# Silu of keys and queries on ScalarE, two tiles to a function table, and a logits bias on TensorE

## The chip, the cores and the metric

The kernel runs on one core of a Trainium2 chip. The metric is the device time of one execution in microseconds. A core has TensorE (PE, matrix products), VectorE (DVE), ScalarE (ACT, activation functions), GpSimd (POOL) and SyncE (SP, which here only starts transfers), and 16 DMA engines. Each engine executes its own instructions in order, and they meet at semaphores.

## The reference, cut to what matters

The input is 8 sequences of 512 tokens of width 256. All arithmetic is in float32.

```
xn = layernorm(x)
# attention branch, 16 heads of 16
q = silu(xn @ Wq)            k = l2_norm(silu(xn @ Wk))       v = xn @ Wv
gamma = -sigmoid(xn @ Wgamma)          f = sigmoid(xn @ Wf1 @ Wf2)
a = k * gamma * f
for each token:  S = S * f ;  sab = a . S ;  S = S + k (sab + v) ;  o = q . S
s = layernorm(o * sigmoid(xn @ Wog1 @ Wog2)) * norm_w @ Wo
# expert branch, 8 experts, top 2
logits = xn @ Wg + bg
out = sum over the two chosen experts of weight * (gelu(xn @ W1 + b1) @ W2 + b2)
g = silu(layernorm(out) * gamma + beta)
result = x + s * g
```

## The kernel before

The 4096 tokens are 32 tiles of 128 partitions; a tile holds 16 consecutive tokens of each of the 8 sequences. The recurrence runs the other way round: 128 partitions hold 8 sequences times 16 heads, and the 512 tokens are taken two by two, as 256 pairs `g`. Eight pairs form a chunk, which is exactly what one tile delivers. Four stages follow each other.

**Head.** Tiles 0 to 3 are projected with nothing beside them.

**Woven stage.** VectorE works the recurrence (`two_steps`), and each of its first pairs carries the VectorE work of one more tile: the pair `g` carries tile `g + 4`. I call such a pair with its tile a slot, and name it by its tile. In a slot VectorE does, in this order: `silu(tile)` (L1009: the product of the projected keys and queries in PSUM, `psA`, with their sigmoid `sg`, into the record `rec`), two wide products and a sum of the recurrence (L1167, L1170, L1172), three more small groups of it, then `scale_k(tile - 1)` (L1024), `square_sums(tile)` (L1015: logits plus their bias; L1019: sums of squares of the keys), then the end of the pair with `scale_a(tile - 1)` (L1031) in it. `scale_a` completes the record of a tile, and SyncE then stores it (`spill`, L368, 768 KB). The stored records come back in the recurrence's layout as chunks (`load_chunk`, L371). SyncE's queue, in order, is for each tile: spill, for the first three a wait for its landing and the load of the chunk, and then a block of zeros (L388) for the expert branch's buffer `xs_d`.

For each tile the other engines do this. TensorE: transposes of the next tile (L827), the low-rank product (L835), keys and queries into `psA` (L841), values, gammas and logits into `psB` (L847), forget and output gates into `psF` (L853). ScalarE (`silus`): normalises the tile after next (`normal`, L624), copies the low-rank product (L646) and the next tile's transposes (L632), takes the sigmoid of `psA` (L652), of gamma (L658), copies the values (L659), takes the sigmoid of the gates (L661), squares the forget gate (L664) and squares the keys (L668). GpSimd (`factors`): forget gate squared times gamma (L474), a maximum (L477), and the power -1/2 (L481) that gives the keys' inverse norm.

`psA`, `psB`, `psF`, the squares and most factors are double-buffered, so tile n waits for tile n-2; the ring `rec` has four places, so tile n waits on `s_recd` until the spill of tile n-4 has landed.

**Routing and scatter.** When slot 32 is done VectorE selects the experts (`route`, L1098 is its last line), GpSimd scatters all token rows to their experts in 64 indirect transfers (L499), and VectorE works on through the recurrence alone up to pair 55.

**Experts beside the shared recurrence.** From pair 56 on GpSimd makes half of the products of each pair (L312, L329), and between pairs it lands the expert outputs in memory (L527) when ScalarE has written them (L719). TensorE runs 39 expert tiles (L887, L899). From pair 224 on, each pair also carries one tile of the output stage (L533 is its first GpSimd step of the expert branch's norm).

The bias of the second expert layer is added by a product of a row of ones with the bias (L901), and the change uses that form.

Of the kernel before, what the change touches and what calls it, by code (L numbers as in the profile page):

```python
# [11 lines left out]
P = 128  # L12
# [41 lines left out]
def build(nc, x, wq, wk, wv, wgamma, wf1, wf2, wog1, wog2, norm_w, wo,  # L54
          wg, bg, w1, b1, w2, b2, gamma, beta, out):
    ctx = ExitStack()
    with ctx:
# [53 lines left out]
        sg = work[:, o1:o1 + 4 * D].rearrange("p (u n) -> p u n", u=2)  # L111
        f2 = work[:, o1 + 4 * D:o1 + 6 * D].rearrange("p (u n) -> p u n", u=2)
        ksq = work[:, o1 + 6 * D:o1 + 7 * D]
# [79 lines left out]
        s_sg = sem("s_sg")  # L193
# [249 lines left out]
        def _(pool):  # L443
# [27 lines left out]
            def factors(n, u, first, last):  # L471
                pool.wait_ge(s_f2, n + 1)
                pool.wait_ge(s_gam, n + 1)
                pool.tensor_tensor(f2[:, u, :].rearrange("p (h c) -> p h c", h=H), f2[:, u, :].rearrange("p (h c) -> p h c", h=H),  # L474
                                   gam[:, u, :].unsqueeze(2).broadcast_to([P, H, HD]), ALU.mult).then_inc(s_fg, 1)
# [5 lines left out]
                pool.tensor_tensor(rinv[:, u, :], ssm[:, u, :], neghalf[:, 0:H], ALU.pow).then_inc(s_ng, 1)  # L481

# [138 lines left out]
        def _(act):  # L621
# [5 lines left out]
            def turned(n, u, first):  # L627
                act.wait_ge(s_T, n + 1)
                if not first:
                    act.wait_ge(s_L, n - 1)  # L630
                    act.wait_ge(s_Bp, n - 1)
                act.activation(xTs[u][:, :, :], psT[u][:, 0:D].rearrange("p (c t) -> p c t", c=KC), ACT.Copy)\  # L632
                    .then_inc(s_xTs, 1)
# [4 lines left out]
            def silus(n, u4, first, last):  # L638
                u = u4 % 2
                first, last, no_record = first and u4 < 2, last and u4 >= RS - 2, first  # L640
                if not last:
                    normal(n + 2)
                act.wait_ge(s_L, n + 1)
                if not first:
                    act.wait_ge(s_Fp, n - 1)
                act.activation(t1[u][:, :], psT[u][0:2 * HD, D:D + P], ACT.Copy).then_inc(s_t1, 1)  # L646
                if not (last and u == 1):
                    turned(n + 1, (u + 1) % 2, first and u == 0)
                act.wait_ge(s_A, n + 1)
                if not first:  # L650
                    act.wait_ge(s_kq, n - 1)
                act.activation(sg[:, u, :], psA[u][:, :], ACT.Sigmoid).then_inc(s_sg, 1)  # L652
                act.wait_ge(s_Bp, n + 1)
                if not first:
                    act.wait_ge(s_rec, n - 1)
                if not no_record:
                    act.wait_ge(s_recd[u4], (n // RS) * 16)
# [656 lines left out]
```

## Time and profile before

| | us |
|---|---|
| median of 3 runs (lowest, highest) | 1235.33 (1234.92, 1239.51) |
| profiled execution, its own time | 1241.86 |
| its span | 1240.1 |
| busy: PE, DVE, ACT, POOL | 941.8, 1122.2, 398.0, 933.0 |
| mean granted clock of TensorE | 0.866 |

The span is the time from the first to the last recorded instruction; busy is the sum over an engine's instructions. VectorE is busy for 90% of the span. The granted clock is 1 at 2.4 GHz and 0.5 at 1.2 GHz. In the timeline views a row begins with its start and its duration in microseconds, and the brackets at its end give the idle time in front of it and what ended that. Two instructions of one engine overlap a little, so the step from start to start is the price of one, and not its duration.

### The profile page before, as it was taken

The numbers are of one execution on the slowest core, as the hardware profiler recorded it, in microseconds if no ns is written. First come the engines' busy times: TensorE is split into PE (matmuls) and PEld (weight loads), VectorE is DVE, ScalarE is ACT, GpSimd is POOL, SyncE is SP. The second block draws the span as 40 slices with busy tenths as digits, with TensorE's granted clock in tenths as the row PEclk, the third lists the DMA queues.
The fourth block names the chain that finished last, engine by engine and source line by source line (L and its number), as shares of the span: only waits on it lengthen the run. The fifth ranks groups of instructions, "written<-read, shape, count | busy, mean of one in ns | idle before, by whom it ended". The sixth has DMA issues, their size and how long they took to land.

```text
span 1240.1 us, 17339 instructions
## 1 busy us (share of the span) xinstructions
PE 941.8 (76%) x3773; PEld 686.6 (55%) x3774; DVE 1122.2 (90%) x3478; ACT 398.0 (32%) x1015; POOL 933.0 (75%) x926
## 2 busy tenths in 40 slices
PE   5888888200019999999999999999999952667663
PEld 2333333100017778888787878887888841445442
DVE  3789999999999999999999999899999999978882
ACT  3444544200003232233223333332332213454552
POOL 3766666447753888888888888888888888777763
PEclk9788989655559999999999999999999985676777
DMA  5565655464333566666566666666666453443322
GB/s 163 171 226 178 188 201 190 147 211 114 108 107 119 174 190 200 195 199 189 181 188 192 199 201 185 185 192 199 199 199 192 131 150 101 111 135 117 83 68 56
DMA packets 238034, 202.59 MB, mean 163 GB/s; under 512 B 140401, under 2 KB 216017, under 8 KB 237969
## 3 DMA queue, kind: packets, MB, share of 16 engines
q1 hardware_dynamic: 160930, 82.81, 25.5%
q10 hardware_dynamic: 70224, 100.49, 24.4%
q0 software_dynamic: 6816, 18.69, 4.5%
q14 instruction: 54, 0.44, 0.1%
q8 instruction: 10, 0.16, 0.1%
HBM read 139.42 MB, written 62.54 MB: 163 GB/s over the span
## 4 chain that ended last, share of the span: by engine, by line
PE 56%; DVE 17%; POOL 8%; DMA 7%; issue 6%; ACT 4%; SPq 3%; ACTq 0%; DVEq 0%; POOLq 0%
PE psF L899 22%; PE psA L887 20%; POOL xs_d L499 6%; PE psA L955 4%; PE psF L901 4%; DMA rec_d<-work 3%; PE psF L917 2%; DMA work<-xs_d 2%; DVE obh L1156 2%; SPq L337 2%; DVE ubuf L1172 1%; PE psT L875 1%; DVE prod_a L1167 1%; DVE work L1009 1%; PE psT L949 1%
## 5 line engine op out<-in xcount | busy, mean ns | idle before, releaser
L312 POOL TENSOR_TENSOR prod_a<-state,rbh 128x512 f32<-128x512 f32 x200 | 254.4, 1272 | 94.0 <-DVE state L1227 68.8
L899 PE MATMUL psF<-wts,work 128*128 128x256 f32 x1248 | 290.0, 386 | 2.3 <-ACT work L708 1.2
L887 PE MATMUL psA<-xT,wts 128*128 128x256 f32 x1248 | 281.9, 385 | 1.3 <-ACT xT L702 0.8
L887 PEld LDWEIGHTS psA<-xT,wts 128*128 128x128 f32 x1248 | 235.6, 191 | 45.0 <-issue 13.8
L899 PEld LDWEIGHTS psF<-wts,work 128*128 128x128 f32 x1248 | 232.3, 191 | 48.1 <-issue 16.8
L329 POOL TENSOR_TENSOR prod_q<-state,rbh 128x512 f32<-128x512 f32 x175 | 221.9, 1268 | 0.0
L1156 DVE TENSOR_REDUCE obh<-prod_q 128x16 f32<-128x272 f32 x512 | 218.7, 428 | 0.0
L708 ACT ACTIVATE work<-psA,b_sb 128x256 f32<-128x256 f32 x312 | 130.7, 470 | 162.4 <-PE psA L887 159.0
L1214 DVE TENSOR_REDUCE ubuf<-prod_a 128x16 f32<-128x272 f32 x200 | 86.1, 431 | 46.5 <-POOL prod_a L312 46.4
L719 ACT ACTIVATE work<-psF,work 128x256 f32<-128x256 f32 x78 | 36.9, 473 | 256.8 <-PE psF L901 245.7
L875 PE MATMUL psT<-ident,work 128*128 128x128 f32 x156 | 24.2, 279 | 118.2 <-DMA work<-xs_d 118.2
L481 POOL TENSOR_TENSOR rinv<-ssm,neghalf 128x16 f32<-128x16 f32 x32 | 100.7, 3148 | 2.7
L499 POOL DMA_INDIRECT xs_d<-x_acc,idx x64 | 79.0, 1234 | 19.5 <-issue 18.9
L527 POOL DMA_INDIRECT y_d<-work,ids x78 | 78.9, 1011 | 14.6 <-issue 12.6
L1227 DVE TENSOR_TENSOR state<-psB,outer 128x256 f32<-128x256 f32 x200 | 84.4, 422 | 5.8
L1206 DVE TENSOR_TENSOR prod_a<-state,psT 128x256 f32<-128x256 f32 x200 | 83.9, 420 | 6.0
L875 PEld LDWEIGHTS psT<-ident,work 128*128 128x128 f32 x156 | 19.3, 143 | 123.9 <-issue 115.3
L1209 DVE TENSOR_REDUCE psB<-prod_a 128x16 f32<-128x272 f32 x200 | 86.8, 434 | 0.0
L1220 DVE TENSOR_TENSOR psB<-prod_a,psB 128x256 f32<-128x256 f32 x200 | 83.8, 419 | 0.0
L1212 DVE TENSOR_TENSOR psB<-rbh,psB 128x256 f32<-128x256 f32 x200 | 83.7, 419 | 0.0
L1222 DVE TENSOR_TENSOR outer<-rbh,psB 128x256 f32<-128x256 f32 x200 | 83.0, 415 | 0.0
L841 PE MATMUL psA<-w_kq,xT 128*128 128x512 f32 x128 | 78.9, 749 | 0.0
(171 smaller groups left out, 1564.0 us busy)
## 6 DMA issues: line engine op xcount, KB each, us to landing
wts<-in_L_ffn_W_dram ACTq DMA_DIRECT2D x78, 1024.0 KB, 5.4
rec_d<-work SPq DMA_DIRECT2D x32, 768.0 KB
rbh<-rec_d SPq DMA_DIRECT2D x32, 768.0 KB, 5.6
xs_d<-zero SPq DMA_DIRECT2D x26, 387.0 KB, 9.2
work<-xs_d ACTq DMA_DIRECT2D x39, 258.0 KB, 5.6
wts<-y_d ACTq DMA_DIRECT2D x16, 512.0 KB, 5.7
x_acc<-in_L_attn_x_dram SPq DMA_DIRECT2D x32, 128.0 KB
o_d<-obh SPq DMA_DIRECT2D x32, 128.0 KB, 7.3
```

The costliest lines, as they stand in the source:

```text
L312: eng.tensor_tensor(prod_a[:, n, 1:3, :, 0:HD], state[:, g % SR, :, :].unsqueeze(1).broadcast_to(wide), rows.unsqueeze(2).broadcast_to(wid ...
L329: eng.tensor_tensor(prod_q[:, g % SR, :, :, 0:HD], state[:, g % SR, :, :].unsqueeze(1).broadcast_to(wide), rbh[:, u, 2 * n - 1:2 * n + 1, ...
L481: pool.tensor_tensor(rinv[:, u, :], ssm[:, u, :], neghalf[:, 0:H], ALU.pow).then_inc(s_ng, 1)
L499: pool.indirect_dma_start(xs_d, bass.IndirectOffsetOnAxis(idx[:, 2 * n + c:2 * n + c + 1], 0), x_acc[:, n, :], None).then_inc(s_sc, 16)
L708: act.activation(hT[:, m, :], psA[m // 2 % 2][:, m % 2 * MT:(m % 2 + 1) * MT], ACT.Gelu, bias=b1_sb[:, bass.ds(e * FC + m, 1)]).then_inc(s ...
L887: mm = pe.matmul(psA[m // 2 % 2][:, m % 2 * MT:(m % 2 + 1) * MT], w1_sb[v][:, c, m * P:(m + 1) * P], xgT[:, c, :], start=(c == 0), stop=(c ...
L899: pe.matmul(psF[q][:, 0:D], hT[:, m, q * P:(q + 1) * P], w2_sb[v][:, m, :], start=(m == 0), stop=False)
L1156: dve.tensor_reduce(obh[:, c % OB, row % RING, :], prod_q[:, g % SR, side, :, :], AX.X, ALU.add).then_inc(s_o, 1)
L1206: dve.tensor_tensor(prod_a[:, n, 0, :, 0:HD], old, over_v(home_a[:, n, :]), ALU.mult).then_inc(s_chain, 1)
L1209: dve.tensor_reduce(u1, prod_a[:, n, 0, :, :], AX.X, ALU.add).then_inc(s_chain, 1)
L1214: dve.tensor_reduce(raw, prod_a[:, n, 2, :, :], AX.X, ALU.add).then_inc(s_chain, 1)
L1227: dve.tensor_tensor(new, home_o, outer[:, 1, :, :], ALU.add).then_inc(s_chain, 1)
```

## The change

VectorE's `silu` and its semaphore go. ScalarE takes the Silu of `psA` itself and writes it to the record (after: L652), and squares the keys behind it (L657). Silu and Sigmoid lie in different function tables, so ScalarE reloads its table (ACT_TABLE_LOAD) between them. To share the reloads the tiles go in groups: tile 0, then 1 and 2, 3 and 4, up to 29 and 30, then 31. In a group the silus of both tiles come first (`ahead`, `silu_kq`), and then the sigmoids of both (`sigmoids`). The loop over tiles is written out. The squares get a second buffer.

The logits' bias becomes a product on TensorE, a row of ones times `bg_bc`, 128x8, added to `psB` (after: L856), and ScalarE copies the logits out (L666). GpSimd makes the inverse norm first and the product with gamma last (L471, L475, then L478). On VectorE `square_sums(tile)` now stands ahead of `scale_k(tile - 1)`.

```diff
 POOL, factors(n):
-                pool.wait_ge(s_f2, n + 1)
-                pool.wait_ge(s_gam, n + 1)
-                pool.tensor_tensor(f2[:, u, :]..., gam..., ALU.mult).then_inc(s_fg, 1)
                 pool.wait_ge(s_ss, n + 1)
                 pool.tensor_scalar(ssm[:, u, :], ss[:, u, :], 1e-24, None, ALU.max).then_inc(s_ssm, 1)
...
                 pool.tensor_tensor(rinv[:, u, :], ssm[:, u, :], neghalf[:, 0:H], ALU.pow).then_inc(s_ng, 1)
+                pool.wait_ge(s_f2, n + 1)
+                pool.wait_ge(s_gam, n + 1)
+                pool.tensor_tensor(f2[:, u, :]..., gam..., ALU.mult).then_inc(s_fg, 1)
 ACT:
-                act.wait_ge(s_A, n + 1)
-                act.activation(sg[:, u, :], psA[u][:, :], ACT.Sigmoid).then_inc(s_sg, 1)
...
+            def ahead(n):
+                if n + 2 < NT:
+                    normal(n + 2)
                 act.wait_ge(s_L, n + 1)
+                if n >= 2:
                     act.wait_ge(s_Fp, n - 1)
+                act.activation(t1[n % 2][:, :], psT[n % 2][0:2 * HD, D:D + P], ACT.Copy).then_inc(s_t1, 1)
+                if n + 1 < NT:
+                    turned(n + 1)
+            def silu_kq(n):
+                u, u4 = n % 2, n % RS
                 act.wait_ge(s_A, n + 1)
+                if n >= RS:
+                    act.wait_ge(s_recd[u4], n // RS * 16)
+                act.activation(rec[:, u4, :, K_:K_ + 2 * HD]..., psA[u][:, :]..., ACT.Silu).then_inc(s_kq, 1)
+                act.wait_ge(s_kq, n + 1)
+                if n >= 2:
+                    act.wait_ge(s_ss, n - 1)
+                act.activation(heads(ksq[:, u, :]), rec[:, u4, :, K_:K_ + HD], ACT.Square).then_inc(s_ksq, 1)
+            def sigmoids(n):
                 act.wait_ge(s_Bp, n + 1)
+                if n >= 2:
                     act.wait_ge(s_rec, n - 1)
                 act.activation(gam[:, u, :], psB[u][:, D:D + H], ACT.Sigmoid).then_inc(s_gam, 1)
                 act.activation(rec[:, u4, :, V_:V_ + HD], heads(psB[u][:, 0:D]), ACT.Copy).then_inc(s_v, 1)
+                act.activation(logits[:, n, :], psB[u][:, D + H:D + H + E], ACT.Copy).then_inc(s_lg, 1)
...
-            per_tile(act, silus, RS)
+            for group in [(0,)] + [(n, n + 1) for n in range(1, NT - 1, 2)] + [(NT - 1,)]:
+                for n in group:
+                    ahead(n)
+                    silu_kq(n)
+                for n in group:
+                    sigmoids(n)
 PE:
-                    mm = pe.matmul(psB[u][:, 0:D + H + E], xTs[u][:, c, :], w_vgg[:, c, :],
-                                   start=(c == 0), stop=(c == KC - 1))
-                mm.then_inc(s_Bp, 1)
+                    pe.matmul(psB[u][:, 0:D + H + E], xTs[u][:, c, :], w_vgg[:, c, :], start=(c == 0), stop=False)
+                pe.matmul(psB[u][:, D + H:D + H + E], ones[0:1, :], bg_bc[0:1, :], start=False, stop=True).then_inc(s_Bp, 1)
 DVE:
-            def silu(n):
-                u, u4 = n % 2, n % RS
-                dve.wait_ge(s_sg, n + 1)
-                if n >= RS:
-                    dve.wait_ge(s_recd[u4], (n // RS) * 16)
-                dve.tensor_tensor(rec[:, u4, :, K_:K_ + 2 * HD]..., sides(psA[u][:, :]), sides(sg[:, u, :]), ALU.mult)
...
-                dve.wait_ge(s_v, n + 1)
-                dve.tensor_tensor(logits[:, n, :], psB[u][:, D + H:D + H + E], bg_bc[:, :], ALU.add).then_inc(s_lg, 1)
                 dve.wait_ge(s_ksq, n + 1)
...
                 if tile is not None:
-                    scale_k(tile - 1)
                     if tile < NT:
                         square_sums(tile)
+                    scale_k(tile - 1)
```

ScalarE, one tile of the woven stage before, as its loop's body has it (`work` stands for `rec`, `sg`, `f2` and `ksq`, which share one buffer; ISA and REGISTER_ALU rows are waits and loop arithmetic):

```order
L624 ACTIVATE x_acc<-x_acc,shift,rstd 128x256
L643 REGISTER_ALU
L645 REGISTER_ALU [waits s_L]
L646 ACTIVATE t1_0<-psT0 32x128 [waits s_Fp]
L632 ACTIVATE xT2<-psT1 128x256 [waits s_Bp,s_L,s_T]
L652 ACTIVATE work<-psA0 128x512 [waits s_kq,s_A]
L657 ISA [waits s_rec,s_Bp]
L658 ACTIVATE gam<-psB0 128x16 [waits s_recd0]
L659 ACTIVATE work<-psB0 128x16x16
L661 ACTIVATE work<-psF0 128x2x16x16 [waits s_Fp]
L664 ACTIVATE work<-work 128x256 [waits s_f]
L668 ACTIVATE work<-work 128x256 [waits s_ss,s_kq]
```

And after, the middle of the group of tiles 3 and 4: the second tile's silu, the reload, and the first tile's sigmoids.

```order
L622 ACTIVATE x_acc<-x_acc,shift,rstd 128x256 [waits s_rstd]
L643 ACTIVATE t1_0<-psT0 32x128 [waits s_Fp,s_L]
L630 ACTIVATE xT2<-psT1 128x256 [waits s_Bp,s_L,s_T]
L652 ACTIVATE work<-psA0 128x2x16x16 [waits s_recd0,s_A]
L657 ACTIVATE work<-work 128x256 [waits s_ss,s_kq]
L664 ACT_TABLE_LOAD [waits s_rec]
L664 ACTIVATE gam<-psB1 128x16 [waits s_Bp]
L665 ACTIVATE work<-psB1 128x16x16
L666 ACTIVATE logits<-psB1 128x8
L668 ACTIVATE work<-psF1 128x2x16x16 [waits s_Fp]
L671 ACTIVATE work<-work 128x256 [waits s_f]
L664 ACTIVATE gam<-psB0 128x16 [waits s_rec,s_Bp]
```

The wait for a spill (`s_recd0`) moved from gamma's sigmoid to the silu, and gamma and the gates of the first tile now stand behind the silu of the second. There are 34 reloads in the whole stage, where there was one.

VectorE, the middle of a slot before:

```order
L1182 TENSOR_TENSOR outer<-rbh,ubuf 128x256
L1024 TENSOR_TENSOR work<-work,rinv 128x16x16
L1015 TENSOR_TENSOR logits<-psB1,bg_bc 128x8
L1019 TENSOR_REDUCE ss<-work 128x16
L1190 TENSOR_TENSOR prod_a<-prod_a,outer 128x16x16
L323 TENSOR_TENSOR prod_q<-state,rbh 128x16x16
L1192 TENSOR_SCALAR prod_q<-ubuf,pair 128x16
L1031 SCALAR_TENSOR_TENSOR work<-work 128x16x16
L1196 TENSOR_TENSOR state<-prod_a,outer 128x256
L1156 TENSOR_REDUCE obh<-prod_q 128x16
L1009 TENSOR_TENSOR work<-psA0,work 128x16x32
L1167 TENSOR_TENSOR prod_a<-state,rbh 128x2x16x16
```

The same stretch after:

```order
L1174 TENSOR_TENSOR outer<-rbh,ubuf 128x256
L1013 TENSOR_REDUCE ss<-work 128x16
L1018 TENSOR_TENSOR work<-work,rinv 128x16x16
L1182 TENSOR_TENSOR prod_a<-prod_a,outer 128x16x16
L321 TENSOR_TENSOR prod_q<-state,rbh 128x16x16
L1184 TENSOR_SCALAR prod_q<-ubuf,pair 128x16
L1025 SCALAR_TENSOR_TENSOR work<-work 128x16x16
L1188 TENSOR_TENSOR state<-prod_a,outer 128x256
L1150 TENSOR_REDUCE obh<-prod_q 128x16
L1159 TENSOR_TENSOR prod_a<-state,rbh 128x2x16x16
```

The wide product with the sigmoid and the small logits sum are gone, and the sum of squares stands directly behind the recurrence's outer product, one place ahead of the key scaling.

## Rows read from the trace of the kernel before

**Rows 1.** The page: the chain of waits that ended last, by engine.
```profile
PE 56%; DVE 17%; POOL 8%; DMA 7%; issue 6%; ACT 4%; SPq 3%; ACTq 0%; DVEq 0%; POOLq 0%
```
**Rows 2.** One window: us, busy PE, PEld, DVE, ACT, POOL, PE's clock, DMA share, GB/s.
```profile
120.00:180.00 60.00, 50.95 (x145) 23.14 (x146) 59.97 (x176) 29.12 (x85) 39.66 (x29) 0.89 0.62 197
```
**Rows 3.** Who waited for whom: us in total, times, longest.
```profile
POOL prod_a L312 <- DVE psT L1133: 23.8, 1, 23.8
```
**Rows 4.** Timeline of GpSimd and ScalarE just before pair 224.
```profile
1003.53 0.47 ACT L719 ACTIVATE work<-psF,work 128x256 f32<-128x256 f32 x1 [3.80 <-PE psF L901]
...
1005.18 1.01 POOL L527 DMA_INDIRECT y_d<-work,ids  x1 [0.17 <-issue]
```
**Rows 5.** Timeline of VectorE over the slot of tile 18.
```profile
143.71 0.68 DVE L1009 TENSOR_TENSOR work<-psA,work 128x512 f32<-128x512 f32 x1
...
144.31 0.68 DVE L1167 TENSOR_TENSOR prod_a<-state,rbh 128x512 f32<-128x512 f32 x1
...
147.71 0.15 DVE L1015 TENSOR_TENSOR logits<-psB,bg_bc 128x8 f32<-128x8 f32 x1
147.79 0.40 DVE L1019 TENSOR_REDUCE ss<-work 128x16 f32<-128x256 f32 x1
...
149.94 0.68 DVE L1009 TENSOR_TENSOR work<-psA,work 128x512 f32<-128x512 f32 x1
```
**Rows 6.** Timeline of TensorE over the same tile, and one product later.
```profile
145.72 1.12 PE L853 MATMUL psF<-w_up,t 32*128 32x512 f32 x2 [1.39 <-ACT t L646]
146.77 0.44 PE L827 MATMUL psT<-ident,x_acc 128*128 128x128 f32 x2
147.70 1.98 PE L841 MATMUL psA<-w_kq,xT 128*128 128x512 f32 x4
149.52 1.11 PE L847 MATMUL psB<-w_vgg,xT 128*128 128x280 f32 x4
...
154.60 3.00 PE L841 MATMUL psA<-w_kq,xT 128*128 128x512 f32 x4
```
**Rows 7.** The bias product's weight load: ns min/median/max.
```profile
L901 PEld LDWEIGHTS psF<-b_sb,ones x156: 180/182/185, 381.6 to 1002.9; 1*128 1x128 f32 x156
```
**Rows 8.** Timeline of ScalarE over one tile.
```profile
149.54 0.18 ACT L658 ACTIVATE gam<-psB 128x16 f32<-128x16 f32 x1 [3.13 <-DVE work L1031]
...
150.84 0.40 ACT L668 ACTIVATE work<-work 128x256 f32<-128x256 f32 x1
...
151.75 0.25 ACT L646 ACTIVATE t<-psT 32x128 f32<-32x128 f32 x1
...
152.17 0.57 ACT L652 ACTIVATE work<-psA 128x512 f32<-128x512 f32 x1
```
**Rows 9.** Timeline of ScalarE at the experts' first table load.
```profile
371.86 1.28 ACT L708 ACT_TABLE_LOAD   x1 [4.03 <-PE psA L887]
373.15 1.57 ACT L708 ACTIVATE work<-psA,b_sb 128x256 f32<-128x256 f32 x4
```
**Rows 10.** GpSimd's inverse norm and gamma product: busy us, mean ns, idle before.
```profile
L481 POOL TENSOR_TENSOR rinv<-ssm,neghalf 128x16 f32<-128x16 f32 x32 | 100.7, 3148 | 2.7
...
L474 POOL TENSOR_TENSOR work<-work,gam 128x256 f32<-128x256 f32 x32 | 21.7, 677 | 5.8 <-ACT work L664 5.6
```
**Rows 11.** The chain in order of time, 40 to 100 us: start, duration, what.
```profile
41.28 8.02 DMA rec_d<-work
...
63.38 15.20 DMA rec_d<-work
78.68 0.69 DVE work L1009
...
85.32 0.60 DVE work L1009
```
**Rows 12.** Timeline: a spill issued behind a chunk's load, and who waited.
```profile
143.14 5.30 SPq L368 DMA_DIRECT2D rec_d<-work  x1
...
157.06 0.18 ACT L658 ACTIVATE gam<-psB 128x16 f32<-128x16 f32 x1 [4.32 <-DMA rec_d<-work]
```

More of the change, by code:

```diff
@@ L110, in build @@
         o1 = RS * H * REC
-        sg = work[:, o1:o1 + 4 * D].rearrange("p (u n) -> p u n", u=2)
         f2 = work[:, o1 + 4 * D:o1 + 6 * D].rearrange("p (u n) -> p u n", u=2)
-        ksq = work[:, o1 + 6 * D:o1 + 7 * D]
+        ksq = work[:, o1 + 6 * D:o1 + 8 * D].rearrange("p (u n) -> p u n", u=2)
         ss = sb("ss", [P, 2, H])
@@ L192, in build @@
         s_Fp = sem("s_Fp")
-        s_sg = sem("s_sg")
         s_gam = sem("s_gam")
@@ L625, in normal, with turned @@
                                scale=rstd[:, bass.ds(n, 1)]).then_inc(s_xn, 1)
-            def turned(n, u, first):
+            def turned(n):
                 act.wait_ge(s_T, n + 1)
-                if not first:
+                if n >= 2:
                     act.wait_ge(s_L, n - 1)
                     act.wait_ge(s_Bp, n - 1)
-                act.activation(xTs[u][:, :, :], psT[u][:, 0:D].rearrange("p (c t) -> p c t", c=KC), ACT.Copy)\
+                act.activation(xTs[n % 2][:, :, :], psT[n % 2][:, 0:D].rearrange("p (c t) -> p c t", c=KC), ACT.Copy)\
                     .then_inc(s_xTs, 1)
@@ L664, in silus @@
                 act.activation(heads(f2[:, u, :]), rec[:, u4, :, F_:F_ + HD], ACT.Square).then_inc(s_f2, 1)
-                act.wait_ge(s_kq, n + 1)
-                if not (first and u == 0):
-                    act.wait_ge(s_ss, n)
-                act.activation(heads(ksq), rec[:, u4, :, K_:K_ + HD], ACT.Square).then_inc(s_ksq, 1)
             for n in range(2):
                 normal(n)
-            turned(0, 0, True)
-            per_tile(act, silus, RS)
+            turned(0)
+            for group in [(0,)] + [(n, n + 1) for n in range(1, NT - 1, 2)] + [(NT - 1,)]:
[4 more added lines that the diff above has]
+                    sigmoids(n)
             act.wait_ge(s_gt, 1)
@@ L1018, in square_sums @@
                     dve.wait_ge(s_ssm, n - 1)
-                dve.tensor_reduce(ss[:, u, :], heads(ksq), AX.X, ALU.add).then_inc(s_ss, 1)
+                dve.tensor_reduce(ss[:, u, :], heads(ksq[:, u, :]), AX.X, ALU.add).then_inc(s_ss, 1)
             def scale_k(n):
@@ L1163, in two_steps @@
                 done = g * CHAIN + 1
-                if tile is not None and tile < NT:
-                    silu(tile)
                 dve.wait_ge(s_chain, done)
@@ L1255, in _ @@
             in_stats(1)
-            dve.wait_ge(s_w, 16 * N_W)
             for n in range(HEAD):
-                silu(n)
                 if n + 2 < len(STATS):
```

25 lines of the change are left out of this document (6 added, 19 removed).

## The prediction

> **What bounds the kernel now.** I read the chain of waits first [rows 1]. More than half of it is TensorE, which points at the expert phase. That is one of two legs of almost the same length, and both start at one place. The waits between engines show the other leg: GpSimd, done with the scatter, stands idle for 23.8 us until VectorE reaches pair 56 [rows 3]. So the recurrence on VectorE, and not the scatter, sets when the shared recurrence begins. At the far end the last expert output is written at 1003.53 and landed at 1005.18, between two pairs that GpSimd works anyway [rows 4]; it was not waited for, but though only 1.2 us after it was ready (1003.53 + 0.47). The two legs run side by side, and both fork at the routing, which VectorE reaches after its last slot. What moves the routing moves both legs; what moved only one would be lost in the other.
>
> So the question is how long the woven stage lasts. In the window from 120 to 180 us VectorE is busy 59.97 of 60 us, ScalarE 29.12 and GpSimd 39.66, and TensorE 50.95 at a granted clock of 0.89 [rows 2]. VectorE paces it. One slot is 149.94 - 143.71 = 6.23 us [rows 5].
>
> **The change part by part.**
>
> VectorE. The silu product costs 144.31 - 143.71 = 0.60 us from start to start, the logits sum 147.79 - 147.71 = 0.08 [rows 5]. Each slot loses 0.68 us and becomes 5.55 us. The reordering of two short instructions costs nothing there: nothing in the slot waits for either.
>
> How much of it counts. Before tile 9 the pace isn't VectorE's. SyncE's queue holds spill, landing, load and zeros one behind the other, and the spill of tile 4, issued at 63.38, lands 15.20 us later, at 78.58; VectorE's silu of tile 8 starts at 78.68 [rows 11]. That transfer stays, and so do the ones ahead of it, which follow each other in SyncE's queue. Where does slot 9 start then? Now silu(8) on ScalarE starts at 78.6, the squares end near 79.6, the reload takes 1.28 [rows 9], tile 7's sigmoids with their square 1.4 (below), GpSimd's product with gamma 0.7 [rows 10], which is 83.3; scale_a(7) and the two instructions behind it (a spill leaves at 143.14, 0.57 before the next slot starts at 143.71, [rows 5, 12]; with scale_a itself 1.0) bring slot 9 to 84.3. Before, the slot began with silu(9), in the chain at 85.32 [rows 11]. So 1.0 us is won by then, of the 3.4 that five slots lose in work. From there 23 tiles, 9 to 31, lose 0.68 each: 15.6. Together 16.6 us.
>
> ScalarE and TensorE. This is where the change can take back what it gives. I follow the ring through both engines for one group. ScalarE's copy t1 of the first tile starts (0.25, [rows 8]); TensorE makes psF, the transposes, the low-rank product and psA of the second tile, 147.70 + 1.98 - 145.72 = 3.96 [rows 6]; silu and squares 0.57 + 0.40 [rows 8]; the reload 1.28 [rows 9]; two sets of sigmoids, each 150.84 - 149.54 = 1.30 [rows 8], with the new logits copy (bounded by gamma's 0.18, I take 0.08) 1.38, so 2.76; the next normalisation, 151.75 - 150.84 - 0.40 = 0.51. Sum 9.73 us for two tiles, against 2 x 5.55 = 11.10 of VectorE. The second reload of a group lies beside the 3.96 us of TensorE, in which ScalarE has only t1, a copy and a silu of its own to do. So the reloads are covered, by 1.4 us for each group.
>
> The bias product. The trace has the same form in L901: two weight loads of 0.18 us each [rows 7]. Eight columns hardly stream, so from 0 (both loads beside running products) to 0.36 us a tile; I take 0.3, as the loads of one row of weights come in a row. TensorE's own work for one tile is 149.52 - 146.77 = 2.75, then 1.11, then 146.77 - 145.72 = 1.05 [rows 6]: 4.9 us, with the bias 5.2, two tiles 10.4. Still under 11.10, by 0.7 us. This cover is thin, and it holds at a clock of 1. psA's product took 1.98 us at one place and 3.00 at another, where the clock was at its lower level for part of it [rows 6]. With a mean clock of 0.89 a fifth of the time is at 1.2 GHz [rows 2]; TensorE had waited for ScalarE 1.39 us just ahead of psF [rows 6]. In the new order TensorE has fewer pauses (0.7 us for two tiles, against about 2 x 1.3), so I expect a higher clock and not a lower one. If a fifth at 1.2 GHz remains, the ring is 9.73 + 0.2 x 3.96 = 10.5, still under 11.10. But single groups in which all of it is slow take 9.73 + 3.96 = 13.7 and push VectorE back. For these I take 1 us off, once behind the stall at tile 8, where TensorE stood still.
>
> Waits that are added. silu_kq(n) waits for the landing of spill n-4, as VectorE did before. Behind it on ScalarE now queue the squares, the reload and the first tile's sigmoids, for which GpSimd and scale_a wait. Record n-4 is complete 0.57 before the end of slot n-3, at 5.0 of its 5.55 us. Take the second tile of a group, m. Its silu can start at landing time L after that. The first tile's last factor is ready 0.57 + 0.40 + 1.28 + 1.38 + 0.7 = 4.3 us later; scale_a(m-1) needs it at 4.5 of slot m, that is 3 x 5.55 + 4.5 - 5.0 = 16.2 us after the record. So L up to 11.9 us is free. A spill issued behind a chunk's load at 143.14 was waited for until 157.06, 13.9 us [rows 12]. There are two such places in the woven stage after tile 9, and VectorE has its preparation of a chunk beside them (slot 20 starts the later for it; I estimate 1.5 to 2 us from eight instructions no longer than the sum of squares' 0.40, [rows 5]), which brings their limit near 13.8. At these I take 1 us each. The other spills from tile 9 on were landed before anyone asked.
>
> GpSimd. The inverse norm takes 3.15 us [rows 10] and now starts before the gamma product instead of behind it, so the keys' factor comes sooner, and the record's last factor 0.7 later. GpSimd's work per tile is unchanged, 3.15 + 0.68 and one small instruction of 5.55 us.
>
> Sum: 16.6 - 1 - 2 = 13.6, rounded 14 us at the routing. Both legs fork behind it and keep it: the scatter, the recurrence to pair 56, the experts and the output stage have the same instructions as before. The profiled execution took 1241.86 us (span 1240.1 and 1.8 around it), so 1228 for one like it. It lies 6.5 us above the median of 1235.33; the difference is taken over to the median: 1221.3.
>
> **What the Trainium skill would say.** The row shows a table load of 1.28 us and the next activation 0.01 us behind its end [rows 9]. "ScalarE: Activation LUTs", section What ACT_TABLE_LOAD costs, adds a drain of about 1.38 us and counts about 2.66 us for each switch to a different set. By that page the ring would be some 1.4 us longer, 11.1 us, as long as two slots, and the gain would shrink towards that of the ring. In that row the engine had stood idle for 4 us, so nothing was in flight and the row can't refuse the drain entirely. I go by the row.
>
> **The rivals.**
>
> 1. VectorE keeps the pace: the forecast, 1221.3, with 1216 to 1226 as its own range (stalls of 0 to 8 us in the place of 3, and the early stretch won or not).
>
> 2. TensorE and ScalarE take over the pace. For it speaks the thin cover (10.4 against 11.1) and that the second tile's silu now stands ahead of the first tile's sigmoids. If a group takes 12.0 us, halfway between its value at full clock and one with all of TensorE's part slow, 12 groups cost 0.9 x 12 = 11 of the 16 us: about 5 won, 1230. Against it speaks that TensorE's pauses get shorter. A reload that in truth costs twice its row ends near here as well.
>
> 3. Slower than before. The place is the silu of the second tile, the mechanism the spill's landing. The stage's transfers, some 197 GB/s at 6.23 us a tile [rows 2], have to pass in 5.55, 221 GB/s. If that makes the landing long for all, 15.2 us as for tile 4 [rows 11] against 11.9 free, each group loses 3.3 us and gains 1.36: 12 x 1.9 = 23 us slower, 1258. It decides from a landing of 13.3 us on. Against it: four spills of the whole stage were seen above 9 us, each with zeros, another spill or a chunk's load ahead of it.
>
> 4. The legs don't keep the gain: the last landings come so close behind the outputs [rows 4] that a delay of the experts alone shows at once. If the scatter or the experts' weights came later relative to the recurrence, GpSimd would wait there, and the gain would be what the experts' leg has, perhaps half: 1228.
>
> **How the numbers follow.** The forecast has 0.62, the second rival 0.17, the third 0.07, the fourth 0.09; the rest, 0.05, is a gain over 19 us, should the early stretch follow VectorE after all (its 3.4 - 1.0 more, and no stalls). A measurement here tells half a per cent, 6.2 us, from no change. Faster by more than that, below 1229.2: all of the forecast, the large gain, two thirds of the fourth and a third of the second, 0.78. Within it 0.14, slower 0.08. The range from 1214 to 1235 leaves out the third rival and the tails.
>
> **What would show it.** Right: a slot of about 5.55 us on VectorE with no wait in it from tile 10 on, slot 9 about 1 us earlier than now, the routing 14 us earlier, and the same distance from there to the end; 34 reloads of 1.28 us; the clock of TensorE in that stage at 0.89 or above. Wrong: VectorE waiting at the sums of squares or at scale_a for ScalarE or GpSimd in most groups (rival 2), ScalarE's reload or silu waiting for a transfer in most groups (rival 3), or GpSimd waiting for expert outputs at the landings (rival 4).

## The result and the profile after

The changed kernel takes 1230.26 us (median of 10 runs, 1224.26 to 1234.5), the one before 1237.03 beside it (10 runs, 1234.06 to 1240.81). The ratio is 0.9945, with a 95% interval of 0.9926 to 0.9965: 6.8 us faster, where 14 were forecast. The profiled execution took 1230.36 us, its span is 1228.6 and the mean granted clock 0.869.

Five places show how the gain builds up. The events are the same ones in both traces.

| event | before, us | after, us | earlier by |
|---|---|---|---|
| scale_a(8) on VectorE | 90.52 | 88.29 | 2.2 |
| scale_a(31), VectorE's last | 240.08 | 232.77 | 7.3 |
| experts' first product | 367.95 | 362.18 | 5.8 |
| last expert output written | 1003.53 | 996.16 | 7.4 |
| end of the span | 1240.1 | 1228.6 | 11.5 |

The gain is complete at scale_a(31) and is kept up to the last expert output, as forecast. The 4.1 us more at the end of the span come from the output stage, which has the same instructions in both kernels; the medians, 6.8 us apart, don't have them, and the profiled execution before was itself 1241.86 us long. It was the stretch from scale_a(8) to scale_a(31) that gave 5.1 us, where 22 x 0.68 less 3, 12.0, had been expected (22 of VectorE's old silus and logits sums lie in it). The chain of waits after, by engine, against [rows 1]:
```profile
PE 56%; DVE 10%; DMA 10%; POOL 9%; issue 6%; ACT 6%; SPq 3%; ACTq 0%; POOLq 0%; DVEq 0%
```
VectorE's share fell from 17 to 10%, ScalarE and the transfers rose. The windows from 60 to 120 and from 120 to 180 us (columns as in [rows 2]):
```profile
60.00:120.00 60.00, 49.65 (x150) 23.39 (x149) 50.57 (x143) 41.74 (x102) 33.62 (x26) 0.89 0.61 203
120.00:180.00 60.00, 55.10 (x177) 26.59 (x176) 58.79 (x168) 44.21 (x105) 42.65 (x29) 0.89 0.63 207
```
ScalarE went from 29 to 44 of 60 us. VectorE no longer is at 59.97: in the second window it misses 1.2 us, and 203 and 207 GB/s are not the 221 of full slots. What VectorE waited for from 48 to 240 us (in total, times, longest):
```profile
DVE work L1025 <- POOL work L478: 6.9, 6, 2.0
DVE ss L1013 <- ACT work L657: 6.0, 2, 5.7
```
The 5.7 us are the stall of before ahead of tile 8, now at the sum of squares of tile 7 (before, VectorE's silu of tile 7 waited 4.19 us for the same landing, and its silu of tile 8 0.38). The six waits for GpSimd's gamma product are new: scale_a needs it, and 5.5 of the 6.9 us come after scale_a(8). One slot without a wait, VectorE's timeline against [rows 5]:
```profile
144.65 0.41 DVE L1025 SCALAR_TENSOR_TENSOR work<-work 128x256 f32<-128x256 f32 x1
...
147.22 0.66 DVE L316 TENSOR_TENSOR prod_q<-state,rbh 128x256 f32<-128x256 f32 x1
147.81 0.42 DVE L1150 TENSOR_REDUCE obh<-prod_q 128x16 f32<-128x272 f32 x1
...
150.43 0.42 DVE L1025 SCALAR_TENSOR_TENSOR work<-work 128x256 f32<-128x256 f32 x1
```
From scale_a to scale_a it takes 5.78 us, not 5.55. The silu and the logits sum are gone, but L316, which otherwise takes 0.41 us, takes 0.66. So there are two losses: waits, and instructions of VectorE that became longer.

**The waits.** The first tile of a group needs its sigmoids, and ahead of these on ScalarE stand the second tile's silu and a reload. All engines around 91.68 us:
```profile
91.68 0.60 ACT L652 ACTIVATE work<-psA 128x512 f32<-128x512 f32 x1 [4.59 <-DMA rec_d<-work]
...
92.74 1.28 ACT L664 ACT_TABLE_LOAD   x1
94.03 0.18 ACT L664 ACTIVATE gam<-psB 128x16 f32<-128x16 f32 x1
...
94.71 1.18 PE L855 MATMUL psB<-w_vgg,xT 128*128 128x280 f32 x4 [2.08 <-ACT logits L666]
...
95.58 0.62 POOL L478 TENSOR_TENSOR work<-work,gam 128x256 f32<-128x256 f32 x1 [4.92 <-ACT gam L664]
...
96.30 0.42 DVE L1025 SCALAR_TENSOR_TENSOR work<-work 128x256 f32<-128x256 f32 x1 [1.97 <-POOL work L478]
```
The spill had been issued at 76.60 and landed 15.0 us later; it is tile 6's, and tile 10's silu needs its place in the ring. ScalarE stood 4.59 us, GpSimd 4.92, VectorE 1.97. ScalarE stood in the same way at 153.76 and at 203.43, 6.56 us each time. What follows at the second of these, first ScalarE's, then TensorE's timeline and the group after:
```profile
203.43 0.60 ACT L652 ACTIVATE work<-psA 128x512 f32<-128x512 f32 x1 [6.56 <-DMA rec_d<-work]
...
206.46 2.11 PE L855 MATMUL psB<-w_vgg,xT 128*128 128x280 f32 x4 [4.70 <-ACT logits L666]
...
212.92 3.78 PE L849 MATMUL psA<-w_kq,xT 128*128 128x512 f32 x4
...
216.74 0.60 ACT L652 ACTIVATE work<-psA 128x512 f32<-128x512 f32 x1 [3.18 <-PE psA L849]
...
221.36 0.42 DVE L1025 SCALAR_TENSOR_TENSOR work<-work 128x256 f32<-128x256 f32 x1 [1.75 <-POOL work L478]
```
psB is free only when ScalarE has copied the logits, which stand behind the late silu. TensorE stood 4.70 us, and behind that its granted clock was 0.50, its lower level of 1.2 GHz:
```profile
213.00:216.70 3.70, 3.70 (x5) 1.63 (x6) 3.70 (x11) 0.53 (x2) 3.26 (x2) 0.50 0.45 166
```
psA took 3.78 us there instead of 1.98 [rows 6], and the next group's silu waited for it. One late landing thus costs twice: once directly (0.65 us at 208.06), and once as an echo some 13 us later (1.75 at 221.36). The landing before 153.76 cost 0.07 directly and 1.11 as an echo at 171.04.

**The longer instructions.** VectorE and GpSimd, the same moment:
```profile
135.53 0.62 POOL L478 TENSOR_TENSOR work<-work,gam 128x256 f32<-128x256 f32 x1
```
```profile
135.14 0.71 DVE L1164 TENSOR_REDUCE ubuf<-prod_a 128x32 f32<-128x544 f32 x1
135.77 0.66 DVE L316 TENSOR_TENSOR prod_q<-state,rbh 128x256 f32<-128x256 f32 x1
136.35 0.42 DVE L1150 TENSOR_REDUCE obh<-prod_q 128x16 f32<-128x272 f32 x1
```
L316 reads two tensors of SBUF and ends 0.25 us late while GpSimd's gamma product reads two as well. I compared each instruction's step to its successor with the shortest of its kind, waits left out: from scale_a(8) to scale_a(31) this adds 4.7 us after and 1.1 before. Of the 4.7, 0.5 are five steps just ahead of a wait, 0.1 each, and belong to the waits. Nearly all the rest are VectorE instructions beside the gamma product, not L316 alone: the small L1170 took 0.54 us instead of 0.22 four times, and L1184 0.60 and 0.61 instead of 0.23.

### The profile page after: what moved, and what is told of

Read it like the earlier page. It is cut to its first block, busy times and chain, and to the rows that moved or that the text cites. A ratio compares the mean times of both kernels' runs of the same rounds, so it can differ in the third digit from the quotient of the medians.

```text
span 1228.6 us, 17343 instructions
## 1 busy us (share of the span) xinstructions
PE 945.2 (77%) x3837; PEld 691.2 (56%) x3838; DVE 1103.6 (90%) x3414; ACT 446.3 (36%) x1080; POOL 929.9 (76%) x926
## 4 chain that ended last, share of the span: by engine, by line
PE 56%; DVE 10%; DMA 10%; POOL 9%; issue 6%; ACT 6%; SPq 3%; ACTq 0%; POOLq 0%; DVEq 0%
PE psF L906 22%; PE psA L894 20%; POOL xs_d L497 6%; DMA rec_d<-work 6%; PE psA L962 4%; PE psF L908 4%; PE psF L924 2%; DMA work<-xs_d 2%; SPq L335 2%; DVE obh L1150 1%; PE psT L882 1%; PE psT L956 1%; ACT gT L788 1%; ACT gw L767 1%; ACT xT L805 1%
## 5 line engine op out<-in xcount | busy, mean ns | idle before, releaser
L894 PEld LDWEIGHTS psA<-xT,wts 128*128 128x128 f32 x1248 | 235.4, 191 | 45.3 <-issue 13.8
L475 POOL TENSOR_TENSOR rinv<-ssm,neghalf 128x16 f32<-128x16 f32 x32 | 96.7, 3022 | 2.7
L710 ACT ACTIVATE xT<-psT 128x512 f32<-128x512 f32 x39 | 23.3, 597 | 146.0 <-PE psT L882 127.5
```

What stands on the lines that cost most here:

```text
L894: mm = pe.matmul(psA[m // 2 % 2][:, m % 2 * MT:(m % 2 + 1) * MT], w1_sb[v][:, c, m * P:(m + 1) * P], xgT[:, c, :], start=(c == 0), stop=(c ...
```

## The experiments

The changed kernel left three theories. A: the landings come too late for the ring of four records, since ScalarE now stands ahead of them with more behind it; what is lost is lost through them. B: ScalarE's tile is too long, above all by its reloads, and the landings only touch it because of that. C, formed after the first runs: GpSimd's gamma product meets VectorE's products of two SBUF tensors. "sa8" and "sa31" stand for the starts of scale_a(8) and scale_a(31), from each kernel's one profile; a slot is the median from one scale_a to the next after sa8. All in one table first; times with an interval are ratios to the kernel before, run beside them on one chip.

| kernel | sa8 | sa31 | slot | ratio (interval) | median us |
|---|---|---|---|---|---|
| before | 90.52 | 240.08 | 6.29 | 1 | 1237.03 |
| after | 88.29 | 232.77 | 5.92 | 0.9945 (0.9926-0.9965) | 1230.26 |
| e11 after, again | 89.05 | 231.89 | 5.91 | 0.9919 (0.9898-0.9940) | 1232.54 |
| e1 ring of 8 | 80.96 | 219.55 | 5.79 | 0.9828 (0.9805-0.9852) | 1221.60 |
| e2 one table | 87.94 | 226.87 | 5.79 | 0.9923 (0.9902-0.9944) | 1231.79 |
| e3 before, logits moved | 89.91 | 238.37 | 6.22 | 1.0016 (0.9997-1.0034) | 1243.83 |
| e4 before, ring of 8 | 86.08 | 235.36 | 6.29 | 0.9980 (0.9962-0.9999) | 1239.45 |
| e5 zeros late | 81.87 | 222.95 | 5.79 | 0.9884 (0.9860-0.9908) | 1226.02 |
| e6 GpSimd's old order | 93.68 | 247.95 | 5.91 | 1.0114 (1.0082-1.0146) | 1254.52 |
| e7 ring of 8, one table | 81.09 | 219.68 | 5.79 | one run | 1223.0 |
| e8 ring of 8, small gamma product | 78.18 | 212.02 | 5.54 | one run | 1211.07 |
| e9 ring of 8, two steps swapped | 80.40 | 216.78 | 5.66 | 0.9818 (0.9796-0.9841) | 1220.07 |
| e10 tiles singly | 89.32 | 230.87 | 6.05 | 0.9938 (0.9912-0.9963) | 1236.31 |

**e1, a ring of eight records** (places 5 to 7 and the squares of gates and keys lie in a buffer that is free until the experts start; the cut shows one line of the edit):
```
-RS = 4
+RS = 8
```


> The changed kernel with eight places in the ring of records in the place of four (five in their old buffer, three in the experts' weight buffer, which is idle in that stage), so that a silu waits for the landing of the spill eight tiles back. The last scale_a starts at 232.8 us in the changed kernel and at 240.1 in the one before; VectorE waits 5.7 us at the sums of squares and 5.5 us at scale_a after tile 8. Theory A (the second tile's silu waits for a spill's landing, and the first tile's sigmoids stand behind it): both kinds of wait mostly go, the last scale_a starts at 223 to 227 us, the time falls by 6 to 9 us against the changed kernel. Theory B (the reloads themselves and TensorE's pace make the waits): the waits behind the landings only turn into waits for psA, the last scale_a no earlier than 230, the time within 3 us of the changed kernel.

Measured: sa31 at 219.55, 13.2 us before the changed kernel's and earlier than any theory had it, 7.3 of them by sa8 and 5.9 behind it. The time, too, is lower by more than the 6 to 9 us of theory A (0.9828 against 0.9919 and 0.9945, 11 to 15 us). From sa8 to sa31 VectorE waits only 0.03 us three times. Its windows, and GpSimd's waits in the shared phase (385 to 1005 us):
```profile
60.00:120.00 60.00, 56.26 (x188) 27.60 (x186) 59.97 (x170) 47.63 (x114) 47.43 (x32) 0.94 0.65 226
120.00:180.00 60.00, 54.51 (x182) 26.73 (x181) 59.97 (x171) 46.56 (x112) 46.87 (x31) 0.94 0.64 211
```
```profile
POOL y_d L533 <- ACT work L735: 8.1, 5, 3.2
```
Theory A holds for the waits: when nothing waits for the landings VectorE is at 59.97 again, and TensorE's granted clock at 0.94. But the slot is still 5.79, so a second cause remains.

**e2, one table** (the sigmoid in the place of the silu, leaving out its product with the input; a single load):
```
-  ... ACT.Silu).then_inc(s_kq, 1)
+  ... ACT.Sigmoid).then_inc(s_kq, 1)
```


> The changed kernel with Sigmoid in the place of Silu for keys and queries, so that the stage needs no reload of the function table; it leaves out the product with the input, and all else is the same. Theory A (landings): 34 reloads of 1.28 us go from ScalarE, but the silus still wait for the landings; the last scale_a moves from 232.8 to 230 or 231, and the time by 1 to 3 us. Theory B (reloads): the waits of VectorE for the gamma product at scale_a (6.9 us) go, the last scale_a starts at 226 to 228, the time falls by 5 to 7 us. A drain of 1.38 us with each reload would show as more than that, over 10 us.

Measured: sa31 at 226.87, as theory B had it. Its waits:
```profile
DVE ss L1013 <- ACT work L657: 5.7, 3, 5.0
...
DVE work L1025 <- POOL work L478: 1.2, 2, 0.6
```
Without reloads ScalarE makes good most of a late landing. Theory B has a part, so far, of 5 to 6 us at sa31 (against e11 and after). In time it had 5 to 7 us and missed: the ratio is within 0.2% of the changed kernel's two, which the intervals don't tell from nothing.

**e7, ring of eight and one table**, both edits at once:
```
-RS = 4
+RS = 8
-  ... ACT.Silu).then_inc(s_kq, 1)
+  ... ACT.Sigmoid).then_inc(s_kq, 1)
```


> Eight places in the ring and Sigmoid in the place of Silu (the product with the input is left out), so neither landings nor reloads are in the way. Theory A says that the reloads matter only where a landing has made ScalarE late: with eight places VectorE waited nowhere, so nothing is left to win, and the last scale_a starts at 219 to 220 us as with eight places alone. If the reloads cost by themselves: 214 to 217.

Measured: 219.68, against e1's 219.55. Where nothing waits for a landing the reloads of the woven stage cost nothing. So B isn't a cause by itself: a reload costs only where a landing has made ScalarE late already. (sa31 is from one profile of each.)

**e3, only the logits, on the kernel before** (bias as a product of one row on TensorE, copy on ScalarE, VectorE's sum gone):
```
+  pe.matmul(psB[u][:, D + H:D + H + E], ones[0:1, :], bg_bc[0:1, :], start=False, stop=True)
-  dve.tensor_tensor(logits[:, n, :], psB[u][:, D + H:D + H + E], bg_bc[:, :], ALU.add)
```


> The kernel before with only the logits' part of the change: bias by a product on TensorE, copy on ScalarE, no logits sum on VectorE. VectorE loses 0.08 us in each of 32 tiles. If VectorE alone paces the stage: the last scale_a at 237.7 in the place of 240.1, the time 2 us lower, 0.2%. If the product on TensorE (0.3 to 0.5 us a tile with its loads) costs: no gain, or up to 3 us slower.

Measured: sa31 1.7 us earlier, where 2.4 had been expected, 0.6 of it by sa8 and 1.1 behind it; the slots are 0.07 shorter, as the row of the sum has it. The time is unchanged (1.0016, up to 1.0034), so the 2 us less that were expected didn't come, and a small cost of the product isn't ruled out. In its profile GpSimd waits for expert outputs at landings in the shared phase:
```profile
POOL y_d L527 <- ACT work L721: 8.9, 5, 2.6
```
**e4, only the ring of eight, on the kernel before** (buffers moved as in e1, and ScalarE's loop over the tiles written out; the cut shows one line):
```
-RS = 4
+RS = 8
```


> The kernel before with the eight-place ring, ScalarE's loop written out. VectorE waited 4.6 us for landings before tile 9, and nowhere after. Theory A, and the account of the early stage: those 4.6 us go, and the last scale_a starts at 235 to 236 in the place of 240.1, the time falls by 4 to 5 us. Together with the ring on the changed kernel this tells how much of the ring's gain is owed to the change. If SyncE's queue of early spills holds the stage in another way (chunk loads): within 1 us.

Measured: sa31 4.7 us earlier, nearly all of it by sa8 (4.4), as expected, and 0.2% of time, 2.5 us where 4 to 5 had been expected. So the kernel before had little to win from a longer ring; it is the changed one that needs it.

**e5, zeros late** (SyncE issues the zeros behind the last tiles and not behind the first):
```
-  if n < ZN:
-      sp.dma_start(xs_z[n], zero[:, :]).then_inc(s_zero, 16)
+  if n >= NT - ZN:
+      sp.dma_start(xs_z[n - (NT - ZN)], zero[:, :]).then_inc(s_zero, 16)
```


> The changed kernel, with the 26 blocks of zeros issued beside tiles 6 to 31 in the place of 0 to 25; all else the same, four places in the ring. If the early landings of 10 and 15 us are long because zeros, spills and chunk loads stand in one line, VectorE's wait of 5.7 us before tile 8 goes, scale_a of tile 8 starts at 82 to 83 in the place of 88.3, and the later waits (5.5 us at scale_a) stay: last scale_a at 227 to 228, time 4 to 6 us below the changed kernel. If the landings are long by themselves: nothing changes before tile 8. The rival has the scatter wait for the last zeros, and gives the gain back there.

Measured: sa8 at 81.87, 6.4 us earlier, and sa31 at 222.95, 4 us better than expected. The stall ahead of tile 8 is gone (0.4 us left) and the waits for gamma are down to two:
```profile
DVE work L1025 <- POOL work L478: 2.3, 2, 1.6
```
The zeros were what made the early landings take 15 us: by the updates of its semaphore tile 6's spill lands in 8.4 us here and took 15.0 in the changed kernel. The late landings behind a chunk's load stay (14.3 us for tile 16's), and cost 2.3.

**e6, GpSimd's old order** (gamma product ahead of the inverse norm):
```
+  pool.wait_ge(s_f2, n + 1); pool.wait_ge(s_gam, n + 1)
+  pool.tensor_tensor(f2[...], f2[...], gam[...], ALU.mult)
   ... the inverse norm of tile n
-  pool.wait_ge(s_f2, n + 1); pool.wait_ge(s_gam, n + 1)
-  pool.tensor_tensor(f2[...], f2[...], gam[...], ALU.mult)
```


> The changed kernel with GpSimd's order of before: gamma product, maximum, inverse norm. The gamma product waits for the forget gates, which the first tile of a group gets late. If the new order is needed: GpSimd's inverse norm starts after that, VectorE waits for it at scale_k in most groups, about 1 to 3 us each, last scale_a 10 us or more later than 232.8, near or above the kernel before. If the order only moves the product: slots as in the changed kernel, last scale_a within 2 us.

Measured: 1.1% slower than before. The norm, which VectorE needs first, stands behind the product that waits for the late sigmoids:
```profile
DVE work L1018 <- POOL rinv L479: 26.9, 9, 6.3
```
The new order was therefore no detail: with ScalarE's silus, it is worth 15 us at sa31. It isn't what makes the gamma product meet VectorE's instructions, though. In the old order the product falls beside VectorE's key scaling, in eight of the 23 slots:
```profile
99.42 0.62 POOL L472 TENSOR_TENSOR work<-work,gam 128x256 f32<-128x256 f32 x1
...
99.49 0.84 DVE L1018 TENSOR_TENSOR work<-work,rinv 128x256 f32<-128x256 f32 x1 [1.34 <-POOL rinv L479]
```
L1018 takes 0.41 us otherwise. By the measure from above, the steps ahead of waits left out, this kernel has 5.4 us of longer instructions.

**e8, ring of eight with a small gamma product** (GpSimd multiplies one head of 16; the product of the others is left out):
```
-  f2[:, u, :].rearrange("p (h c) -> p h c", h=H)
+  f2[:, u, :].rearrange("p (h c) -> p h c", h=H)[:, 0:1, :]
```


> Eight places in the ring, and GpSimd's product of forget gates and gamma on 16 of 256 columns; it leaves out that product for the other heads. With eight places the slots last 5.67, 5.79 and 6.24 us, 5.80 in the mean, where 5.60 was worked out, and VectorE's two-operand instructions are up to 0.35 us longer where they meet that product. Theory C (the two engines keep each other off while both read SBUF): the slots fall to 5.60, one like the other, last scale_a 4 us earlier, near 215.5. Rival (the length comes from semaphores and waits in VectorE's own queue): slots stay at 5.67 to 5.8.

Measured: slot 5.54, sa31 at 212.02 (215.5 had been expected; 2.8 of the difference to e1 are there by sa8), and the longer instructions add up to 0.1 us. From sa8 to sa31 it takes 133.84 us, e1 138.59: 4.75 less, and the longer instructions of e1 added up to 4.7. The same place as above, VectorE's timeline in e1 and in e8:
```profile
108.06 0.66 DVE L324 TENSOR_TENSOR prod_q<-state,rbh 128x256 f32<-128x256 f32 x1
```
```profile
104.16 0.71 DVE L1172 TENSOR_REDUCE ubuf<-prod_a 128x32 f32<-128x544 f32 x1
104.78 0.42 DVE L324 TENSOR_TENSOR prod_q<-state,rbh 128x256 f32<-128x256 f32 x1
```
**e9, ring of eight, the work whole, two steps of VectorE swapped** (a one-operand sum stands where the gamma product falls, the two-operand product behind it):
```
+  sum_row(g - 2, 0), moved ahead of
   if g > 0:
       read_left(dve, g)
```


> Eight places in the ring, and in each slot VectorE's sum of one operand (sum_row of two pairs back) put ahead of its product of two operands (read_left), so that GpSimd's gamma product, which started 0.24 us before that product in eight of the slots from tile 8 on and made it 0.66 us long, now meets an instruction that reads SBUF once. Theory C (only instructions that read two operands from SBUF are held up): those eight keep 0.42 us, 2.0 of the 4.4 us of lengthening go, slots of 5.54 to 5.66 where there were 5.79, last scale_a 217 to 218 us (219.6 without the swap); the time at most 2 us lower than with eight places alone, against which no median can tell it. Rival (GpSimd holds up any instruction): the sum becomes as long, nothing moves.

Measured: sa31 at 216.78; the longer instructions add 2.5 us instead of 4.7, and the stretch takes 2.2 us less than in e1 (136.38). GpSimd's and VectorE's timeline:
```profile
107.01 0.62 POOL L486 TENSOR_TENSOR wts<-wts,gam 128x256 f32<-128x256 f32 x1
```
```profile
107.25 0.42 DVE L1158 TENSOR_REDUCE obh<-prod_q 128x16 f32<-128x272 f32 x1
107.60 0.41 DVE L324 TENSOR_TENSOR prod_q<-state,rbh 128x256 f32<-128x256 f32 x1
```
The sum, which reads one tensor, isn't touched by it: theory C holds, and its rival, that GpSimd holds up any instruction, doesn't. This is the fastest kernel that does all the work: 0.9818. That it beats e1 is seen at sa31 of one profile each (2.8 us), not in the times, whose intervals overlap.

**e10, tiles singly** (each a group of its own, so 64 loads and not 34):
```
-  for group in [(0,)] + [(n, n + 1) for n in range(1, NT - 1, 2)] + [(NT - 1,)]:
+  for group in [(n,) for n in range(NT)]:
```


> The changed kernel with every tile a group of its own: 64 reloads in the place of 34, but no sigmoid waits behind another tile's silu. ScalarE's own work for one tile becomes 3.9 us with its logits copy, and 2.56 of reloads, 6.5 us, over the 5.6 to 5.8 of a slot of VectorE. If the count of reloads decides, ScalarE sets the pace, slots of 6.5 us, last scale_a 10 to 18 us later than 232.8, slower than the kernel before. If the coupling of two tiles was the worse: slots under 6, last scale_a at or below 232.

Measured: sa31 at 230.87, as the second theory had it (at or below 232), and far from the first, 10 to 18 us later; the median slot of 6.05 us is a little over the 6 of the second and well under the 6.5 of the first. In time it is no slower than the pairs (0.9938 against 0.9919 for e11 beside it, intervals overlapping). In eight of the 23 slots ScalarE sets the pace, with two reloads in each 6.04 us; its timeline from 174 to 187 us has no idle time:
```profile
178.01 1.28 ACT L652 ACT_TABLE_LOAD   x1
...
180.36 1.28 ACT L664 ACT_TABLE_LOAD   x1
...
184.05 1.28 ACT L652 ACT_TABLE_LOAD   x1
```
but no second tile's silu stands ahead of the first one's sigmoids, and the waits at gamma are gone. Going by pairs saves 1.3 us of ScalarE's time a tile and, as I read it, gives it back through the landings.

**e11, the changed kernel again**, on e9's and e10's chip:

> The changed kernel unchanged, beside the others on their chip. If the waits of its first profile are its own and not that execution's: last scale_a within 1.5 us of 232.8, VectorE's wait before tile 8 of 5 to 6 us and 4 to 7 us of waits at scale_a; ratio to the kernel before 0.993 to 0.996, so that eight places are worth 1.0 to 1.3% more and the later zeros 0.5 to 0.8%.

Measured: sa31 at 231.89, within the 1.5 us that were expected, and a ratio of 0.9919, a little below the 0.993 to 0.996. The same kinds of wait are there:
```profile
DVE work L1025 <- POOL work L478: 6.1, 5, 1.5
DVE ss L1013 <- ACT work L657: 5.7, 1, 5.7
```
Behind both chunk places direct cost and echo come again: 0.97 us at 157.94 and 1.21 at 170.70, then 0.07 at 207.50 and 1.42 at 220.47. The 1.97 us behind tile 8 don't come again (0.06 at 95.12). After sa8 the waits are 3.7 us here and 5.9 in the first profile, so their size differs by some 2 us from one execution to the next.

## Why the prediction was right in direction and wrong in size

**VectorE's two instructions: right.** From sa8 to sa31 they stand 22 times each, which takes 22 x 0.60 + 22 x 0.076 = 14.9 us. e8, with nothing else in the way, takes 133.84 us for the stretch and before 149.56: 15.7 less, of which 1.1 are the longer instructions of before. That leaves 14.6 for the 14.9.

**The early stretch: better than forecast.** Slot 9 was to start 1.0 us earlier. It starts at 83.42 instead of 85.25 (its first instruction in VectorE's timeline), 1.8 earlier. 0.3 of the difference is a slip in my sum: 79.6 + 1.28 + 1.4 + 0.7 is 83.0 and not 83.3. The rest is that silu(8) started at 77.74 and not at 78.6: tile 4's spill had landed sooner. At scale_a(8), in the middle of slot 9, 1.0 + 0.68 = 1.7 had been expected and 2.2 are found.

**The ring through ScalarE and TensorE: right.** I had 9.73 us for a group of two tiles. Where the group follows closest upon the one before, from the load at 172.52 to the load at 182.63, it takes 10.11.

**The landings: the step was named, its price too low.** I had allowed a landing of 11.9 us, 13.8 beside a chunk's preparation, and priced one slow group behind tile 8 and two chunk places with 1 us each. Measured are 1.97 + 0.32 at the first and 1.11 + 0.65 + 1.75 at the others: 5.8 instead of 3. Two things failed. "The other spills from tile 9 on were landed before anyone asked" was read from the kernel before, where tile 6's spill landed in 10.4 us by the updates of its semaphore; now it takes 15.0, and it is asked for 10.5 us after its issue, at 87.1. And I took each late landing to act once. At the chunk places the direct cost, 0.07 and 0.65, was within the 1 us each; but the logits copy stands behind the landing as well, psB stays occupied, TensorE idles and its clock is granted at 0.50 afterwards, and the next group pays 1.11 and 1.75. The echo is read from the chain of rows, and e11 has it again. e1 shows the whole from the other side: its landings take 8 to 20 us, nobody waits for them, the clock is 0.94, and the stretch is 5.9 us shorter.

**"GpSimd's work per tile is unchanged": this is what failed besides.** The work is unchanged, what it meets isn't. With the silus on ScalarE the gamma product falls beside VectorE's two-operand instructions more often and at worse moments, and that costs 4.7 - 1.1 = 3.6 us. e8 takes the product away and brings it to nothing; e9 moves VectorE's instruction and gets half back; e6 shows that GpSimd's old order has it too. A cost of this kind had no term in my sum. The rule of the Trainium skill ("SBUF — State Buffer", section Who interferes with whom) is that a VectorE instruction with two SBUF inputs contends with a GpSimd one that reads SBUF, and that one with a single input doesn't, outside the modes that take both of VectorE's ports. L316 and the sum of e9 agree with it; L1184, which reads one tensor and one number for each partition, was held up too (0.60 us), so the rows leave open what else counts. I had not weighed the rule.

The account: 13.6 forecast, plus 0.5 (early), less 2.8 (waits), less 3.6 (longer instructions) is 7.7; found are 7.3. The experiments close it without the forecast: the changed kernel's stretch of 144.5 us is e8's 133.8, plus the 4.75 that e1 has over e8 and the 5.9 that the changed kernel has over e1.

**The reloads: right, with a condition.** 34 loads of 1.28 us, hidden where nothing waits for a landing (e7 against e1), not where one is late (e2: 5 to 6 us at sa31). For the drain that I had weighed there is now a row with work directly in front of the load:
```profile
182.25 0.36 ACT L630 ACTIVATE xT<-psT 128x256 f32<-128x256 f32 x1
182.63 1.28 ACT L652 ACT_TABLE_LOAD   x1
183.92 0.60 ACT L652 ACTIVATE work<-psA 128x512 f32<-128x512 f32 x1
```
The load starts 0.02 us behind the copy's end, and the silu 0.01 behind the load's. There's no drain of 1.38 us in it. By an estimate from the drain in "ScalarE: Activation LUTs" of the Trainium skill (What ACT_TABLE_LOAD costs) e10 would need 2.8 us more for each tile than its 6.04. The measurement decides: no drain is paid here.

**The bias product** stood at 0.3 us; TensorE's own row is 0.38 at full clock and 0.59 at the lower (L856), and from its start to the next product's 0.25 (88.44 to 88.69). e3 shows no cost of it in VectorE's slots, which are shorter by the sum's 0.07.

**Both legs keep the gain: right, within a few us.** Over the timed kernels, what sa31 gains and what the time gains go together: 7.3 and 6.8 for after, 8.2 and 8.6 for e11, 20.5 and 20.3 for e1, 23.3 and 21.1 for e9, 17.1 and 15.4 for e5, 13.2 and 10.1 for e2, 4.7 and 2.5 for e4, 9.2 and 4.8 for e10, 1.7 and -2 for e3, -7.9 and -13 for e6 (times against the runs of before beside them). Rival 4's mechanism exists, as e1's and e3's rows of GpSimd's waits show, and takes 0 to 9 us in single profiles. It doesn't follow the gain: e6, the latest at sa31, has 8.2 us of such waits, e8, the earliest, 0.7, and the two profiles of the changed kernel 0 and 5.7. Whether it or chance between executions takes the 2 to 5 us that lack in some of these stays open: each of them has one profile.

**The rivals.** 2 and 3 each had a part of the mechanism (ScalarE in front of the landing, the lower clock) but at three places and not in most groups. Neither was the cause of more than 2.8 of the 6.3 us that were missing at sa31. No rival held the contention, and no slot of the changed kernel reached the 5.55 us that were to show the forecast right; e8's median, 5.54, does. The third rival's argument, that only four spills of the stage took over 9 us, was a misreading: by the updates of their semaphores 18 of the 32 did, 14.5 us the longest of them behind a chunk's load.

## What to carry to other kernels

When an engine gets work that waits for a transfer, list all that now stands behind that wait, the copies that free a buffer for TensorE too: a late landing is paid there once more, with a lower clock. And when an edit shifts one engine's instructions by a microsecond, look at what of it now falls beside what of VectorE: GpSimd's two-operand work belongs beside sums of one tensor (PSUM operands were not tried). Try the ring's length together with the change, since the same ring was worth 0.2% on the kernel before and about 1% on the changed one (0.9828 against 0.9919 and 0.9945).

## What the runs showed of the hardware

- A VectorE instruction of two SBUF tensors (0.41 us) took 0.66 when GpSimd's product of two (0.62 us) had started 0.24 us ahead of it; a sum of one tensor at the same place kept its 0.42. GpSimd's product is held up in its turn: it took 1.49 us where it overlapped L1018, L1182, L321 and L1184 (108.56).
- A table load took 1.28 us in all kernels, behind running work too, and 64 of them instead of 34 left the time as it was.
- After it had waited 4.70 us TensorE's clock was granted at 0.50 over the window from 213.00 to 216.70, though it was busy for all 3.70 us of it; psA took 3.78 us, otherwise 1.98.
- By the updates of its semaphore, a spill of 768 KB landed in 7.5 to 15.6 us in the changed kernel and in 7.5 to 20.0 with eight places in the ring (e1), where no engine waited for one from sa8 on.
